# Router logits made token by token, the shared expert as a fifth chunk of the inner layer, and identity turns at two more waits of TensorE, in a fused attention and mixture-of-experts kernel

## The reference, cut to what matters

```
scores = sigmoid(x @ gate_W) * route_scale            # 8 experts, two are kept
topk_scores, topk_idx = top_k(scores, 2);  topk_w = topk_scores / topk_scores.sum(-1)
h = gelu(einsum('bsd,edh->bseh', x, W1) + b1);  y = einsum('bseh,ehd->bsed', h, W2) + b2
expert_out = einsum('bse,bsed->bsd', gate_full, y)
shared = gelu(x @ Ws1 + bs1) @ Ws2 + bs2
return expert_out + shared
```

## Time and profile before

| | |
|---|---|
| median of 3 runs | 303.39 us (302.92 to 304.26) |
| the profiled execution | 304.41 us, of which the span in the profile is 302.7 us |
| busy share of the span | PE 82%, DVE 79%, ACT 64%, POOL 28% |
| mean granted TensorE clock | 0.949 of full speed |

### The profile page before, as it was taken

One profiled execution on the slowest core, in us unless ns is written; L12 is line 12 of the kernel. 1 busy time (PEld: TensorE's weight loads), 2 busy tenths in 40 slices (PEclk: granted clock), 3 DMA queues, 4 the chain that ended last, 5 costly groups with the idle time before them and its releaser, 6 DMA issues.

```text
span 302.7 us, 4600 instructions
## 1 busy us (share of the span) xinstructions
PE 248.6 (82%) x1559; PEld 170.7 (56%) x1559; DVE 240.0 (79%) x573; ACT 192.6 (64%) x458; POOL 84.4 (28%) x145
## 2 busy tenths in 40 slices
PE   5756875788499879998888799989897897699893
PEld 5334351777164538777644367778454586584383
DVE  6299989976986699679988699599967997817743
ACT  1681067227849964798788845898698334375851
POOL 4923000004307011222764103025641131230013
PEclk9989599599979979999999989999999799999999
DMA  7406831001979930304999820108899701000003
GB/s 212 112 0 177 250 88 34 0 2 27 226 226 219 198 73 0 96 10 77 239 241 218 182 45 0 37 0 163 240 234 212 153 0 35 2 0 2 2 5 99
DMA packets 22945, 31.32 MB, mean 103 GB/s; under 512 B 3893, under 2 KB 17038, under 8 KB 22922
## 3 DMA queue, kind: packets, MB, share of 16 engines
q1 hardware_dynamic: 20330, 21.59, 24.7%
q0 software_dynamic: 2592, 9.44, 17.8%
HBM read 5.07 MB, written 2.10 MB: 24 GB/s over the span
## 4 chain that ended last, share of the span: by engine, by line
PE 42%; ACT 26%; DVE 21%; POOL 5%; issue 4%; DMA 1%; POOLq 0%; DVEq 0%; ACTq 0%
PE psH L1263 7%; PE psA L1183 5%; PE psF L1322 5%; PE psY L1358 4%; DVE prods L940 4%; ACT xn L645 3%; PE psA L1231 3%; ACT xn L555 3%; DVE prods L269 3%; PE psA L1358 3%; ACT squares L638 3%; POOL rstd L435 2%; PE psY L1212 2%; PE psA L1175 2%; POOL var L433 2%
## 5 line engine op out<-in xcount | busy, mean ns | idle before, releaser
L269 DVE TENSOR_TENSOR prods<-qT,kT 128x1024 f32<-128x1024 f32 (+1 forms) x44 | 49.3, 1176 | 3.8 <-ACT qT L541 3.8
L433 POOL TENSOR_SCALAR var<-ss 128x4 f32<-128x4 f32 (+1 forms) x25 | 11.7, 470 | 137.6 <-ACT squares L631 64.9
L1263 PE MATMUL psH<-ident,prods 128*128 128x128 f32 x324 | 42.8, 284 | 0.0
L1263 PEld LDWEIGHTS psH<-ident,prods 128*128 128x128 f32 x324 | 39.1, 148 | 2.3 <-issue 2.3
L940 DVE TENSOR_TENSOR prods<-v_shift,prob 128x896 f32<-128x896 f32 x32 | 34.7, 1083 | 0.0
L1063 DVE TENSOR_TENSOR hid<-hid,psG 128x512 f32<-128x512 f32 x32 | 20.8, 683 | 16.0 <-PE psG L1344 15.4
L435 POOL TENSOR_TENSOR rstd<-var,neg_half 128x4 f32<-128x4 f32 (+2 forms) x28 | 32.3, 1155 | 2.3
L1322 PE MATMUL psF<-x3T,w 128*128 128x512 f32 x58 | 31.0, 646 | 0.4 <-ACT gexp L659 0.3
L1231 PE MATMUL psA<-prods,slot_sel 128*32 128x512 f32 x168 | 24.7, 636 | 6.9 <-DVE prods L269 5.6
L1183 PE MATMUL psA<-xnT,wqkv 128*128 128x512 f32 x48 | 26.2, 683 | 3.3 <-ACT xnT L541 3.3
L940 DVE TENSOR_TENSOR prods<-v_tok,prob 128x128 f32<-128x128 f32 (+2 forms) x60 | 20.7, 372 | 0.0
(11 more groups left out here) (213 smaller groups left out, 561.6 us busy)
## 6 DMA issues: line engine op xcount, KB each, us to landing
v_shift<-v_tok SPq DMA_DIRECT2D x20, 448.0 KB
convT<-tapT POOLq DMA_DIRECT2D x9, 512.0 KB, 5.1
x_in<-L_attn_x SPq DMA_DIRECT2D x4, 512.0 KB, 3.7
x_res<-L_attn_x SPq DMA_DIRECT2D x4, 512.0 KB, 10.3
out<-y_out SPq DMA_DIRECT2D x7, 256.0 KB, 2.3
v_shift<-v_tok SPq DMA_DIRECT2D x4, 384.0 KB
tapT<-tapT POOLq DMA_DIRECT2D x3, 512.0 KB, 9.2
convT<-kexp POOLq DMA_DIRECT2D x3, 512.0 KB, 7.6
```

What stands on the lines that cost most here:

```text
L269: return eng.tensor_tensor(prods[:, QUADS * (s % 2) + q, t0:T], qT[:, t0:T], kT[:, PRE - off + t0:PRE - off + T], ALU.mult)
L1263: ins = pe.matmul(dst, terms[:, j % TERM_BUFS, m, :], ident[:], is_transpose=True, start=False, stop=(m == live[-1]))
```

## The change

The logits are made directly in token-major form: for each tile of 128 tokens, `x3T` is the stationary operand and the 8 router columns of `w1` stream past it, so that the result is already 128 tokens by 8 experts. C4, its copy to `gate_shared` and the turn back are gone. The shared expert becomes chunk 4 of `hidden`: PE makes the whole fifth block again into a `psF` bank, and ACT takes Gelu of rows 64 to 127 from PSUM. In batches 1 to 3 chunk 4 of `u0` stands behind `low`, and that of `u1` with chunks 2 and 3 ahead of `sum_terms` 2. Two new groups of identity turns stand at waits: 10 before the turn of x3 of units 2 and 4, and 6 before the logits of units 1, 3 and 5. One of the tail's three groups of 5 is gone.

```
-N_FRONT = 3
-N_HIDDEN = 4
-X3, C4, LOGITS = range(N_FRONT)
+N_FRONT = 2
+N_HIDDEN = CH
+X3, LOGITS = range(N_FRONT)
+FILL_X3, FILL_LOGITS = 10, 6
-LAST_BANKS = (0, 1, 2, 3, 0, 1, 2, 0)
+LAST_BANKS = (0, 1, 2, 3, 0, 1, 2, 0, 1, 2)
...
 (ScalarE)
             def gate_logits(u):
                 act.wait_ge(front_full, upto(u, N_FRONT, 2))
-                copy(gate_shared[:, half_cols(u)], front(u, C4)).then_inc(front_free, 1)
-                act.wait_ge(front_full, upto(u, N_FRONT, 3))
...
-                    nc.scalar.activation(hid[:, c, half_cols(u)], hidden_bank(u, c), ACT.Gelu,
-                                         bias=b1c[:, c:c + 1]).then_inc(hidden_free, 1)
-            def shared_hidden(u):
-                nc.scalar.activation(hid[HID:P, 4, half_cols(u)], gate_shared[HID:P, half_cols(u)], ACT.Gelu,
-                                     bias=bs1c[HID:P, :]).then_inc(shared_ready, 1)
+                    rows = slice(HID if c == CH - 1 else 0, P)
+                    nc.scalar.activation(hid[rows, c, half_cols(u)], hidden_bank(u, c)[rows, :], ACT.Gelu,
+                                         bias=(bs1c[rows, :] if c == CH - 1 else b1c[:, c:c + 1])).then_inc(hidden_free, 1)
...
-                        hidden(u0, range(2, 4))
-                        shared_hidden(u0)
+                        hidden(u0, range(2, CH))
...
 (ScalarE, tail)
-                    shared_hidden(u0)
+                    hidden(u0, range(0, 1))
                     gates_expert_major(u0)
-                    hidden(u0, range(0, 4))
+                    hidden(u0, range(1, CH))
                     gate_rows(u0)
-                    hidden(u1, range(0, 4))
+                    hidden(u1, range(0, CH))
                     gates_expert_major(u1)
-                    shared_hidden(u1)
...
 (TensorE)
+                if 0 < u < 2 * B - 2 and u % 2 == 0:
+                    keep_busy(FILL_X3, front(u, X3))
                 pe.wait_ge(xn3_ready, u + 1)
...
             def gate_logits(u):
                 if 0 < u < 2 * B - 1:
                     pe.wait_ge(hidden_free, upto(u, N_HIDDEN, 0))
+                if u < 2 * B - 2 and u % 2:
+                    keep_busy(FILL_LOGITS, front(u, LOGITS))
                 pe.wait_ge(front_free, upto(u, N_FRONT, 1))
-                pe.matmul(front(u, C4), w1[:, 4 * P:5 * P], x3T[:, half_cols(u)], start=True, stop=True).then_inc(front_full, 1)
-
-            def turn_logits(u):
-                pe.wait_ge(front_free, upto(u, N_FRONT, 2))
                 for n, j in enumerate(unit_tiles(u)):
-                    ins = pe.transpose(front(u, LOGITS)[:, bass.ts(n, EXPERTS)], gate_shared[0:EXPERTS, bass.ts(j, P)],
-                                       ident[0:EXPERTS, 0:EXPERTS])
+                    ins = pe.matmul(front(u, LOGITS)[:, bass.ts(n, EXPERTS)], x3T[:, bass.ts(j, P)],
+                                    w1[:, 4 * P:4 * P + EXPERTS], start=True, stop=True)
...
                     low(b)
+                    if ffn:
+                        hidden(u0, (4,))
...
                         gate_logits(u1)
                         spread_gates(u0, range(2, 4))
-                        turn_logits(u1)
...
                             if j == 2:
-                                hidden(u1, range(2, 4))
+                                hidden(u1, range(2, CH))
```

More of the change, by code:

```diff
@@ L201, in block_kernel @@
         x3T = sb("x3T", [P, T])
-        gate_shared = sb("gate_shared", [P, T])
         gexp = sb("gexp", [P, TPH, EXPERTS])
@@ L280, in front @@
                 return psF[:, psF_bank(u, use), :]
-            return psY[:] if use == C4 else psH[:]
+            return psH[:]
         def last_chunk(u, c):
@@ L999, in gates @@
                     if n == 0:
-                        dve.wait_ge(front_free, upto(u, N_FRONT, 3))
+                        dve.wait_ge(front_free, upto(u, N_FRONT, N_FRONT))
                     if n or u:
@@ L1310, in hidden @@
                     k = last_chunk(u, c)
-                    if k in (2, 3):
-                        pe.wait_ge(front_free, upto(u + 1, N_FRONT, 2))
-                    elif k > 3:
+                    if k >= CH - 1:
                         before = max(i for i in range(k) if LAST_BANKS[i] == LAST_BANKS[k])
                         pe.wait_ge(hidden_free, upto(2 * B - 2, N_HIDDEN, before + 1))
-                    elif k >= 0:
-                        pe.wait_ge(front_free, upto(u, N_FRONT, N_FRONT - k))
-                    elif c >= 2:
+                    elif c < 2:
+                        pe.wait_ge(front_free, upto(u, N_FRONT, c + 1))
+                    elif k < 0:
                         pe.wait_ge(hidden_free, upto(u, N_HIDDEN, c - 1))
-                    else:
-                        pe.wait_ge(front_free, upto(u, N_FRONT, c + 2))
                     pe.matmul(hidden_bank(u, c), w1[:, bass.ts(c, P)], x3T[:, half_cols(u)],
@@ L1350, in experts_out @@
                     pe.wait_ge(low_used, u // 2 + 2)
-                pe.wait_ge(hidden_free, upto(u, N_HIDDEN, 4))
-                pe.wait_ge(shared_ready, upto(u, 2, 2))
+                pe.wait_ge(hidden_free, upto(u, N_HIDDEN, N_HIDDEN))
+                pe.wait_ge(shared_ready, u + 1)
                 for n in tiles:
@@ L1388, in _ @@
                     linear_state(b, b == 0)
-                    if ffn:
-                        turn_logits(u0)
                     sum_heads(b, 1)
@@ L1454, in _ @@
                     gate_logits(u1)
-                    keep_busy(FILL_FRONT, spare)
-                    turn_logits(u1)
                     hidden(u0, range(2, 4))
```

## The result

The changed kernel takes **308.19 us** (median of 4 runs, 307.93 to 309.31); the kernel before, run beside it, 303.66 (302.92 to 304.26). The ratio is 1.0152, 95% interval 1.0111 to 1.0193: slower by 1.5%, where 300.3 and faster had been forecast. The profiled executions stand at 308.27 us (span 306.5) and 304.41 (302.7), so the two spans show 3.8 of the 4.5 us. Medians here are over all runs; ratios leave out the few runs that lie more than 1.5% above the fastest of the same kernel.

A forecast was written before the change was run, and what follows sets the result against it. No engine's total bounds the kernel; handovers between PE, ACT and DVE decide. Batches 1 to 3 and tail, -1.15 - 0.8 + 1.05 - 0.45 = -1.35, with the clock's -1.7 gave -3.05: median 303.39 to 300.3 us, range 299.0 to 301.6.

The forecast's parts named there:

- the ten turns: Fronts of batches 2 and 3: turns before the turn of x3 make x3T 0.95 and 0.7 us later.
- The logits of u1: Batches 1 and 2: logits made under table load and exp, only gexp left before xnT; -0.97 us each.
- den of batch 3: Batch 3: second gated products and den come about 1.05 us later, and DVE leads from there.
- Batch 1 in sum: -2.0 + 0.86: Batch 1: project_k starts 2.0 us earlier, chunk 4 of u1 adds 0.86; -1.15 in sum.
- the -1.25 ahead of it: Batch 1's front: turn_scores begins near 96.0 instead of 97.25, so DVE's softmax and all behind come 1.25 us earlier.
- The sign of being wrong that I had named: Prediction wrong if batch 1's turn_scores is not earlier against the batch start, or the clock falls in new places.
- I take one of the two falls as gone: Clock falls before project_k in batches 1 and 2, 1.74 us each: one gone, -1.7 us, of 0 to 3.5.
- My rival of dead weight: Turns are dead weight; clock falls anew in fronts of units 2 and 4: 304.9 us, up to 305.5; chance 0.09.
- Chunk 4 of u1 lies under that lead: Batch 3: chunk 4 of u1 is hidden under DVE's lead; batch 3 +1.05 us, +1.6 if it shows.
- Batch 2, -0.8: Batch 2: -1.65 us at project_k, chunk 4 of u1 +0.86; -0.8 in sum.
- My fourth rival: ACT's lead lost to POOL's statistics or DMA sums in batches 1 and 2, chunk 4 paid five times: 303.4; chance 0.09.
- Tail, -0.45: Tail: earlier gexp of u7 and gT of u6 bring the first experts_out to 286.6 instead of 287.07; -0.45 us.

The follow-up runs named there:

- h2: The whole changed kernel with 20 identity turns added ahead of x3 of unit 0; 306.25 us, ratio 1.0077.
- h1: The kernel before with 20 identity turns ahead of x3 of unit 0 and nothing else; 301.94 us, ratio 0.9957.
- g3: The kernel before with 20 identity turns ahead of x3 of unit 0 and six ahead of C4 of units 1, 3 and 5; 299.87 us, 0.9904.
- e1: The changed kernel without its two new groups of identity turns (ten and six); 306.78 us, ratio 1.0122.
- f1: The changed kernel with chunk 4 of u1 behind the turned gates on PE and ACT, and 30 identity turns ahead of batch 3's experts_out(u0); 304.16 us, 1.002.
- e3: The changed kernel without the six turns ahead of the logits of units 1, 3 and 5; the ten stay; 308.31 us, ratio 1.0157.
- e5: The changed kernel with 36 identity turns ahead of experts_out(u0) of batch 3 alone; 307.6 us, ratio 1.0129.
- f3: f1 without the ten turns ahead of x3 of units 2 and 4, but with 20 ahead of x3 of unit 0; 301.29 us, 0.9939.
- f4: The kernel before with ten turns ahead of x3 of units 2 and 4 and six ahead of C4 of units 1, 3 and 5; 304.43 us, 1.0026.
- e4: The changed kernel with chunk 4 of u1 moved from sum_terms 2 to sum_terms 4, ahead of the turn of the gates; 306.22 us, ratio 1.0076.
- f2: f1 without the ten turns ahead of x3 of units 2 and 4; 302.86 us, ratio 1.0003.
- g1: f3 with six identity turns also ahead of the logits of units 2 and 4; 300.72 us, ratio 0.9934.

## Why the prediction was wrong, point by point

**Where the difference lies.** Against the forecast, batch 1 missed by 1.90 us (+0.75 for -1.15), batch 2 by 1.22, batch 3 by 3.59, the tail by 0.68, and the clock's 1.7 did not come as a gain: 9.1 us. Batch 0, which the change leaves alone, gave 2.3 of them back by chance in the profiled execution.

**What held.** Eight logits pairs take 0.96 us behind other work, for 0.89 forecast, and the ten turns bring x3T 1.1 later in batch 2 and 0.8 in batch 3, for 0.95 and 0.7. The logits of u1: gT to `xnT` went from 4.96 to 3.86 and 3.87, -1.10 for -0.97. den of batch 3 is +1.31 for +1.05. `gexp` and gT of the tail are right. Both low stretches before `project_k` went in this execution, and PEclk shows it.

**"Batch 1 in sum: -2.0 + 0.86", which ran along PE and ACT to `project_k`.** This step failed in structure. I followed the chain to `xnT` and took all that lies behind as PE's. It is PE's only while the clock is low. DVE's den comes 5.07 us ahead of `experts_out`, and den waits for the second gated products; gT to den was 4.52 before and is 4.67 now. And gT came 0.70 and 0.35 *later* in batches 1 and 2, where -1.05 and -0.7 were forecast: chunk 4 costs +0.64 of its 0.86 between scores and gT in both batches, where 0.2 and 0.15 were forecast, and in batch 1 the -1.25 ahead of it did not come (scores +0.06). With the front at full clock (h2 against h1) the scores are 1.03 earlier, so that step was right but for the clock. (The sign of being wrong that I had named, `turn_scores` of batch 1 not earlier, is this one: it starts 22.82 after `v_tok`, before 22.54.) Four kernels give the rest, as the distance from den to `experts_out` in batch 1: old form and low clock 6.32, old form and full clock 5.08 (g3), new form and low clock 5.27 (e1; 5.06 in f1 and h2), both 5.07. Early logits and a full clock buy the same microsecond; I added them. This holds for low stretches of 3.4 us; where one of 6.8 lies over `project_k` the distance is 6.60 (e3) and 7.30 (h1).

**The clock, "I take one of the two falls as gone".** Both went in this execution, and were worth at most 1.25 us each and not 1.74. What was missing is where low stretches turn up instead: the one in batch 1's front is 6.8 us long, and that of batch 3 moved from chunks with slack to `experts_out` (+2.23, taken away by e5). My rival of dead weight had the sign and a third of the size (304.9 to 305.5), but neither its place, the fronts of units 2 and 4, nor its mechanism: the 36 turns of e5 and the 20 of f3 did hold the clock. For the six turns it is less clear. In the ten profiles of kernels that have them, `project_k` of batch 1 took 1.98 us in seven and 2.87 to 3.68 in three (f1, f4, h2); that of batch 2 took 1.98 in three (the changed kernel, e4, g3), 2.51 in e5 and 3.35 to 3.78 in six. In the four profiles without them it took 2.98 to 3.78 in both batches. The Trainium skill ("TensorE: Matmul & The Clock Gate", Part 4: PE-mode transpose) says of full clock that it "doesn't engage for transpose-mode"; e5 and f3 disagree, with PEclk at 1.00 through the 36 turns of e5 and the product behind them, no low stretch behind the 20 of f3 in batch 1's front, and 4.63 against 6.96 us for the same product.

**"Chunk 4 of u1 lies under that lead".** This is the step that cost most. In batch 3 the chunk does not lie under DVE's lead; it ends it. I had priced its product and not its bank, which is emptied by a Gelu that stands on ACT behind `y_out` and POOL. With the fall over `experts_out` this is +3.33; f1 takes both away and has 3.31 back. e4, which puts the chunk two tiles later and leaves the clock low, gains 1.94 us in batch 3; e5, which holds the clock and leaves the chunk, 1.78. They add up to more than the whole, so neither gain is one cause's alone. Elsewhere the chunk costs 1.05 for 0.86.

**Batch 2, -0.8.** Measured +0.42: `experts_out` -0.74, with den +0.51 and the distance behind it -1.25; and from there +1.16. The ten turns were the mis-sized term: I let ACT's lead hide them, and the scores came 1.55 later with them than without (e1). My fourth rival had named POOL's statistics, and in batch 2 ACT did wait for them. f2 shows 1.15 in batch 2 and 0.8 in batch 3 without them.

**Tail, -0.45.** Measured +0.22 to the first `experts_out`; the handovers from gT on were taken 0.6 too short. No run isolates which.

**What stays open.** The groups of e4's runs lie 2 us apart, and the runs of e1, e3 and e5 spread more. The mean clock differs between executions of one kernel (0.944 to 0.970 in e5's four runs), so the low stretches do too, and a profile shows one execution of each kernel. So the terms above are those of one execution. That of the chunk's place (2.0) and that of batch 1's front (1.9) are held up by medians of 10 and 12 runs against 4 of the changed kernel; that of the ten turns is near the noise. What the tail's missing group of five turns does was not run. Whether g3 is faster than g1 is not shown, as the intervals overlap; that the rewriting gains nothing beside the same kind of turns is all that these two say.

## What to carry to other kernels

Where a chain runs through one engine only because its clock was low there, ask which engine waits right behind it, and measure from *that* engine's last input to the next product: this distance (5.07 us here) is what a gain upstream must beat. A product that is moved or added takes a bank as well as time: follow the bank to the instruction that empties it, and that engine's list back to what it waits for. Ask of an added product also which slack it uses up: here a slow `experts_out` cost 0.13 us while DVE's work covered it, and was passed on once chunk 4 hung on its end. Identity turns paid where TensorE waited 2.35 us (20 of them, from f2 to f3: 2.65 us in the batch, 1.6 in the median) and cost about their length where it didn't wait (0.8 and 1.15 for ten). After each such edit the low stretches must be looked for anew, since they lay elsewhere in each profile.

## What the runs showed that I had not expected

- Eight pairs with 8 streamed columns took 1.88 us at 1.2 GHz, against 1.06 for the same place in f3: nearly the full factor, though so little streams.
- A low stretch came in lengths of 3.4, 6.8 and 10.2 us, and one that begins after a wait of TensorE can lie on quite other products than the wait (237.9 to 244.8 in batch 3, over `experts_out`, which starts at 240.1).
- POOL's power of 128x8 took 1.67 us before, 2.57 in e1 and 2.72 after, with the same operands; ACT waited 1.09, 0.30 and 1.91 us behind it. Its neighbours on DVE differ; no run isolates why.
